# Recurrent scans: four of a chunk's sixteen key-value products made by GpSimd from a copy that ScalarE takes out of TensorE's bank

## The reference, cut to what matters

```
def step(s, rkvw):
    r_t, k_t, v_t, w_t = rkvw
    a = k_t[..., :, None] * v_t[..., None, :]
    out = jnp.einsum('bhi,bhij->bhj', r_t, u * a + s)
    s = a + w_t[..., :, None] * s
    return (s, out)
```

## Time and profile before

| | |
|---|---|
| median of 3 runs | 3312.01 us (3310.67 to 3313.16) |
| the profiled execution | 3310.44 us |
| its span | 3308.6 us |
| VectorE busy in the span | 2017.9 us (61%) |
| GpSimd busy in the span | 652.9 us (20%) |

### The profile page before, as it was taken

How to read it: one execution, slowest core, us unless ns; L and a number is a source line. 1 busy time by engine, 2 the same in 40 slices (tenths; PEclk the granted TensorE clock), 3 DMA queues, 4 the chain that set the end, 5 groups by cost and what they waited for, 6 DMA issues and landing times. The chain is left out here.

```text
span 3308.6 us, 63547 instructions
## 1 busy us (share of the span) xinstructions
PE 2864.8 (87%) x18753; PEld 1516.3 (46%) x18753; DVE 2017.9 (61%) x4196; ACT 1415.6 (43%) x3023; POOL 652.9 (20%) x482
## 2 busy tenths in 40 slices
PE   5799999999999999999768887599999987788885
PEld 3344444444444444444334444356666655444442
DVE  4667676777677677677367887244444441168774
ACT  2255555555555555555513221254444443221221
POOL 5221222122112212221023332000000000033331
PEclk7699999999999999999979998699999998899996
DMA  6333433343243334333010000111110100100000
GB/s 198 102 89 105 119 108 83 111 116 104 81 120 107 106 88 120 107 98 78 15 62 0 1 0 0 47 34 33 27 33 27 33 15 28 59 0 0 1 0 23
DMA packets 117152, 205.18 MB, mean 62 GB/s; under 512 B 39681, under 2 KB 84463, under 8 KB 116463
## 3 DMA queue, kind: packets, MB, share of 16 engines
q1 hardware_dynamic: 116846, 201.08, 21.3%
HBM read 156.09 MB, written 44.59 MB: 61 GB/s over the span
## 5 line engine op out<-in xcount | busy, mean ns | idle before, releaser
L589 DVE CUSTOM_DVE_ANT_0 masked<-ps_a,mask 112x750 f32<-112x750 f32 x1024 | 941.9, 936 | 378.5 <-PE ps_a L476 369.6
L549 ACT ACTIVATE probs<-ps_a 128x448 f32<-128x448 f32 (+1 forms) x1536 | 743.3, 542 | 547.4 <-PE ps_a L442 543.5
L476 PE MATMUL ps_a<-ks,q_row 96*112 96x375 bf16 x2048 | 529.6, 342 | 57.5 <-DVE part_max L589 34.8
L442 PE MATMUL ps_a<-q_sc,ks 99*128 99x448 bf16 (+1 forms) x1536 | 450.3, 359 | 50.3 <-ACT probs L549 28.5
L462 PE MATMUL ps_a<-probs,vp 128*32 128x224 f32 x6144 | 380.5, 366 | 1.2 <-ACT probs L549 0.9
L476 PEld LDWEIGHTS ps_a<-ks,q_row 96*112 96x112 bf16 x2048 | 220.4, 133 | 330.0 <-issue 271.7
L2014 DVE CUSTOM_DVE_ANT_0 f_masked<-ps_c,f_mp 112x432 f32<-112x432 f32 x256 | 145.6, 606 | 218.2 <-PE ps_c L1866 218.2
L442 PEld LDWEIGHTS ps_a<-q_sc,ks 99*128 99x128 bf16 (+1 forms) x1536 | 132.7, 100 | 283.2 <-issue 234.9
L239 POOL CAST k_piece<-kv_t 64x1500 bf16<-64x1500 f32 x32 | 45.6, 1426 | 1043.3 <-ACT kv_t L231 1043.1
L462 PEld LDWEIGHTS ps_a<-probs,vp 128*32 128x32 f32 x6144 | 164.8, 111 | 158.7 <-ACT probs L549 59.1
L218 PE MATMUL ps_a<-ctx_t,wkv 128*128 128x375 f32 x512 | 197.7, 512 | 20.5 <-DVE x_nat L350 10.8
(11 more groups left out here) (283 smaller groups left out, 3977.9 us busy)
## 6 DMA issues: line engine op xcount, KB each, us to landing
ctx_t<-in_ctx_t SPq DMA_DIRECT2D x32, 1500.0 KB, 8.9
ks<-k_scr SPq DMA_DIRECT2D x64, 562.5 KB, 5.1
mask<-in_mask SPq DMA_DIRECT2D x64, 328.1 KB, 5.4
k_scr<-k_piece SPq DMA_DIRECT2D x64, 281.2 KB, 6.6
k_scr<-k_piece SPq DMA_DIRECT2D x64, 187.5 KB, 6.8
f_context<-in_ctx_t SPq DMA_DIRECT2D x32, 375.0 KB, 3.1
k_scr<-k_piece SPq DMA_DIRECT2D x64, 93.8 KB, 7.1
q_row<-q_scr SPq DMA_DIRECT2D x64, 84.0 KB, 4.5
```

Of the source, the lines that this page charges most:

```text
L442: mm = pe.matmul(out, ks[par][:, j, at], q_sc[par][:, j], start=True, stop=not with_mask)
L476: mm = pe.matmul(ps[0:2 * L, bank + i, 0:SC], q_row[which][:, j, h, gp * 2 * L:(gp + 1) * 2 * L], ks[which][0:SROWS, j, at], start=True, s ...
L549: act.activation(probs[t % 2][0:n, i], ps[0:n, k % SCORE_BANKS, 0:PW] .rearrange("p (h n) -> p h n", h=2), ACT.Exp).then_inc(probs_done, 1)
L589: dve.tensor_tensor_reduce(out=masked[:, u % 2], in0=two_banks(bank, 2 * L), in1=in_two(mask[which][:, c * SU:(c + 1) * SU]), scale=1.0, s ...
```

## The change

The products 2, 6, 10 and 14 of a chunk leave VectorE. ScalarE copies the bank of `vb(i)` to a new SBUF tile `vb` with two buffers, and GpSimd multiplies that by `kt` into the same `kv` buffer. TensorE's bank is then free when the copy is done, and scan `i` waits for GpSimd's product. ScalarE has the four copies at fixed places: the first ahead of the feed-forward reads of the chunk before, the second behind them, the third and fourth around the reads of the turned tile `xt`. GpSimd has product 2 ahead of `rs(0)` and the others ahead of `rs(i - 3)`.

```diff
+POOL_KV = (2, 6, 10, 14)
+DVE_KV = tuple(i for i in range(KC * HS) if i not in POOL_KV)
...
+                def spread_values(c, i):
+
+                    n = len(POOL_KV) * c + POOL_KV.index(i)
+                    act.wait_ge(made["vb"], 16 * c + i + 1)
+                    if n >= 2:
+                        act.wait_ge(s["kv_pool"], n - 1)
+                    act.activation(vb[:, n % 2], ps[:, bank["vb", i, c], 0:N], ACT.Copy).then_inc(s["vb_copied"], 1)
...
                     for i in range(KC * HS + 1):
-                        if i < KC * HS:
+                        if i in DVE_KV:
                             k, j = divmod(i, HS)
...
-                            dve.wait_ge(used["vb"], 16 * c + m + 1)
+                            wait_kv(dve, used["vb"], s["kv_pool"], c, m)
...
+                def products_of(c, i):
+
+                    k = i // HS
+                    n = len(POOL_KV) * c + POOL_KV.index(i)
+                    pool.wait_ge(s["vb_copied"], n + 1)
+                    if i >= 3:
+                        pool.wait_ge(s["state"], 16 * c + i - 2)
+                    pool.tensor_tensor(by_batch(kv[:, i % 3]), kt[:, k, :, 0:L], by_batch(vb[:, n % 2]), ALU.mult)                        .then_inc(s["kv_pool"], 1)
+
                 def read_outs(c):
 
                     pool.wait_ge(used["rec"], 2 * (c + 1))
+                    products_of(c, POOL_KV[0])
                     for m in range(KC * HS):
+                        if m + 3 in POOL_KV:
+                            products_of(c, m + 3)
```

More of the change, by code:

```diff
@@ L722, with wait_kv @@
 CHUNKS_R = B // CB
+POOL_KV = (2, 6, 10, 14)
+DVE_KV = tuple(i for i in range(KC * HS) if i not in POOL_KV)
+def wait_kv(eng, by_dve, by_pool, c, i):
+    if i in POOL_KV:
+        eng.wait_ge(by_pool, len(POOL_KV) * c + POOL_KV.index(i) + 1)
+    else:
+        eng.wait_ge(by_dve, len(DVE_KV) * c + DVE_KV.index(i) + 1)
 def product_order(xt_at):
@@ L801, in rwkv @@
         kv = sb("kv", [P, 3, N])
+        vb = sb("vb", [P, 2, N])
         state = sb("state", [P, 3, N])
@@ L823, in rwkv @@
                  "sxa sxb xx part mixed state rs ruk sq grs og xk2 xr2 "
-                 "sx2a sx2b kk x2 dec_w g_th summed").split()
+                 "sx2a sx2b kk x2 dec_w g_th summed vb_copied kv_pool").split()
         s = {n: sem(n) for n in names}
@@ L859, in room @@
                         name, i, c = before[unit]
+                        if name == "vb":
+                            return wait_kv(pe, used["vb"], s["vb_copied"], c, i)
                         pe.wait_ge(used[name], PRODUCTS[name] * c + i + 1)
@@ L1031, in _ @@
                     now, more = c >= 0, n < CHUNKS_R
+                    if now:
+                        spread_values(c, POOL_KV[0])
                     if more and after_layer0:
@@ L1035, in _ @@
                         ffn(c - 1)
+                    if now:
+                        spread_values(c, POOL_KV[1])
                     if more:
                         deviation(n, 1, 0)
+                        if now:
+                            spread_values(c, POOL_KV[2])
                         turned(n, "xt", xn, "ln1_w", "ln1_b")
+                    if now:
+                        if not more:
+                            spread_values(c, POOL_KV[2])
+                        spread_values(c, POOL_KV[3])
                     if now:
```

## The result

| | kernel before | changed kernel |
|---|---|---|
| median of 12 runs | 3310.07 us | 3317.33 us |
| lowest, highest | 3299.45, 3313.16 | 3305.49, 3320.22 |
| profiled execution's span | 3308.6 us | 3316.7 us |

The ratio is 1.0022, with a 95% interval of 1.0013 to 1.0031: 7.3 us more where 28 were forecast. The direction was right and the size was not. That 3317 lies inside the stated range of 3314 to 3356 is no merit of the sum: it was four times too large.

What follows compares the result with a forecast made beforehand. Scans were taken as bound by turns with GpSimd's instructions: GpSimd 1.13 + scan 0.95 + semaphore 0.08 us a step. Eight phases' delays of 2.5 to 5.4 us summed to 28.1 us; 3312.0 + 28 = 3340 us, range 3314 to 3356.

Steps and rivals of the forecast that it cites:

- product 2 delays `rs(0)`, its sum and `fr`: Start of d1: `rs(0)` waits behind GpSimd's product 2, TensorE's sum of state 0 and `fr` follow late, +1.2 us.
- product 6 delays scan 6: In d1: late `vb(6)`, copy and product push back `rs(3)`, so scan 6 ends at 3026.6 against 3024.92.
- a product under `rs` is worth nothing when it is removed: Scan phases: removing a VectorE product covered by GpSimd's `rs` saves nothing; where no `rs` runs, 0.53 us.
- Added on GpSimd ... 1.13 us: Scan phases: 32 products added on GpSimd at 1.13 us each, 4.5 us a chunk; bounds 0.90 to 1.4 without being held.
- the walk: Step-by-step shifting of d1's timeline, repeated for the other scan phases: +2.5 to +5.4 us each, 28.1 us in all.
- Between the phases nothing changes: Stretches between the eight scan phases: no change in time, so the phases' 28.1 us is the whole cost.
- its clock lowered for longer: Scan phases, part of the worse rival: TensorE waits more and its lowered clock adds 1 to 2 us a chunk.
- the forecast case: Whole kernel: 3322 to 3350 us, from the product's duration bounds and 1 us a chunk of walk error; chance 0.66.
- Absorbed: Rival, scan phases: the lag finds VectorE in unshared work, a chunk pays under 1 us, 3312 to 3319 us; chance 0.12.
- Faster: Rival, scan phases: all four products find gaps in VectorE's scans, 2 us gained a chunk, 3296 us; chance 0.11.
- worse: Rival, scan phases: the strided product takes 1.4 us or TensorE's clock is lowered for longer, 3350 to 3362 us; chance 0.11.
- A rule as a rival: Scan phases: only part of GpSimd's instruction, say half, keeps a scan out, 3326 us; counted within the forecast case.

Runs made afterwards that it cites:

- idle matmuls: Kernel before plus two matmuls, results overwritten, behind the sums of states 13 and 14 per chunk: 3297.88 us, ratio 0.9965; changed kernel plus the same: 3322.61 us, 1.0038.
- only_b: Changed kernel with the four products on GpSimd in layer b only, layer d's left on VectorE: 3317.95 us against 3310.96 before, ratio 1.0022.

## Why the prediction was wrong

**Right.** The mechanism inside a phase. A scan waits for GpSimd's instruction, whoever waits goes next, product 2 delays `rs(0)`, its sum and `fr` (+1.3 us in d1, forecast 1.2), product 6 delays scan 6 (3026.66, forecast 3026.6). The last `rs` of d1 came 1.8 us late, forecast 2.5. GpSimd's product took 1.05 to 1.14 us where it was not held, against an assumed 1.13, ScalarE's copy 0.544 against 0.54. That a product under `rs` is worth nothing when it is removed was not tested by itself.

**The step that failed first: "Added on GpSimd ... 1.13 us", as the price of every GpSimd instruction in the walk.** It is the price of one that starts on a semaphore. One that stands in line ends 0.93 us after the scan, and the step falls from 2.16 to 1.88 us. That is worth 0.6 us up to scan 10 of d0. The phases cost 16.2 us, not 28.1, and this step is a part of the difference; how large a part the runs do not split.

Another part is TensorE's clock inside the phases, for which the walk took the rows of one execution. In d0 TensorE idled 5.26 us before, and the `vb` behind it took 1.81 us; in the changed kernel it idled 0.83 us and the `vb` took 0.98, and VectorE's waits for `vb` there fell from 1.62 and 0.66 us to 0.59. That and the 0.6 us make 2.3 of the 3.9 us between +2.6 and -1.3; the rest is not split. Where the clock fell in another place (the changed kernel with idle matmuls) d0 is 0.8 us longer than before, 2.1 more than here. d1 and d2 had two slow `vb` before and one now: against the d1 of `only_b`, with one, the changed kernel's d1 is 3.2 us longer and not 1.8. So some 5 of the 11.9 us that the phases stayed below the forecast are the clock's.

b1 (+4.5) and b2 (+2.1; forecast 5.4 each) also differ by the clock. GpSimd's product 10 fell in different places, but that alone cost them alike. The four `xhat` of b1, then of b2, in the changed kernel:

```profile
1832.54 2.92 DVE L1127 TENSOR_SCALAR b_xhat<-x_nat,b_rstd,b_shift 128x256 f32<-128x256 f32 x4
...
1932.78 1.38 DVE L1127 TENSOR_SCALAR b_xhat<-x_nat,b_rstd,b_shift 128x256 f32<-128x256 f32 x4
```

and TensorE's two parts of `vb` number 11 a little later, in b1, then in b2 (L942 is the 8-column part at its head):

```profile
1838.03 0.60 PE L942 MATMUL ps_b<-b_s,b_ident 128*128 128x8 f32 x2 [4.89 <-DVE b_rv L1208]
1838.48 1.81 PE L944 MATMUL ps_b<-b_vt,b_vsel 128*128 128x440 f32 x2
...
1935.80 0.39 PE L942 MATMUL ps_b<-b_s,b_ident 128*128 128x8 f32 x2 [1.76 <-DVE b_rv L1208]
1936.04 1.24 PE L944 MATMUL ps_b<-b_vt,b_vsel 128*128 128x440 f32 x2
```

In b1 GpSimd's product 10 held the normalising, in b2 it came after it; but in b2 the last two instructions of `add_ffn` were held instead (2.92 us for 1.28), and scan 10 ends 36.6 us after the first scan in b1 and 36.5 in b2. Then `vb` 11 and 12 are slower in b1, and its scan 11 ends 1.3 us later. So far as the place of product 10 counted, it was probably by the gap that it left TensorE, 4.89 us or 1.76. The other 1.1 us of the difference lies in the kernel before, whose b1 ran with one slow `vb` and whose b2 with two. Taken together the two phases cost 6.7 us where the walk had 10.8; what it charged too much there stays open.

**The step that failed second: "Between the phases nothing changes."** It does: 0.3 to 1.8 us come back behind seven of the eight phases, and in seven `yo` comes 0.8 to 1.3 us sooner after the last `rs` than before (in b0 0.8 later). I had let the clock enter as a danger only ("its clock lowered for longer"). It went up: a line of GpSimd instructions feeds TensorE more evenly (at the end of d1 its waits of 2.3 and 1.7 us became one of 1.4), and the idle matmuls show that the kernel before was losing some 9 to 13 us to this. From 16.2 us in the phases, 5.8 are back by `yo`, 5.5 between phases of one layer, and 1.6 and 1.4 behind the last phase of each. Of the forecast's 28 us this is the larger miss: 14.3 us, against 11.9 in the phases.

What is left is 2.0 us, with 0.5 more ahead of d0 and 0.1 ahead of b0 2.6 (layer b 3.8 longer, layer d 1.2 shorter), and the middle, identical code, is 5.5 us longer in this one execution. The timing over 12 runs says 7.3 (4.3 to 10.3). Where the 2 to 8 us lie that the timing has above the 2.6 of the layers stays open.

**The sums.** The bounds named for the forecast case, 1.4 us for a product and 1 us a chunk, give 3357 and not 3350 as its upper end. And "0.92 to 0.95 in these phases" leaves out b0, which ran at 0.83 before and at 0.87 now. Neither changes the outcome.

**The rivals.** *Absorbed* gave 3312 to 3319 and the time fell there, but for another reason: the lag was not hidden, it was paid and given back by the clock, which is luck for whoever held that view. *Faster* and *worse* did not come about. *A rule as a rival* stays refuted: a scan is held by the whole instruction (the longest, 2.00 us, has nearly a whole `rs` and its own 0.95 us in it). In all thirteen traces no product from a bank took over 0.62 us, while the products from the copy took up to 1.45. The Trainium skill says (SBUF — State Buffer, "Who interferes with whom") that a VectorE instruction with at most one SBUF input, outside its 2-port modes, does not contend with GpSimd; the traces agree.

## What to carry to other kernels

Busy shares do not tell whether work moved to an idle engine is free. Look at which instructions exclude each other: here VectorE's read of a PSUM operand ran beside GpSimd for nothing, and moving it made a holder of it. When a step changes the gaps in which TensorE idles, read the durations of the matmuls behind it: an engine that waits less may also run faster afterwards, and a few matmuls whose result is overwritten can be worth more (9 to 13 us here) than the change under study. And before a difference of 1 or 2 us between two traces is explained, see how far identical stretches of other traces differ: here by up to 1.5 us, with one `vb` at half speed more or less.

## What the runs showed of the hardware that I had not expected

- GpSimd's 448-column two-operand instruction costs 1.13 us from a semaphore and 0.93 us behind a scan that it already waited for.
- Idle gaps of 2.3 and 1.7 us between TensorE's sums are followed by matmuls at half speed; with gaps of 0.80 and 0.17 us they are not. In the changed kernel one gap of 1.4 us alone did not do it. The gap alone does not decide: one of 2.15 us in d0, behind the same instructions, was followed by full speed in the changed kernel and by half speed (granted clock 0.50) in the same kernel with idle matmuls.
- A product moved to GpSimd cost 0.5 us in the phases for the first 32, and another GpSimd instruction beside each 1.35 us.
